# Feed-forward stage: the output tiles of the former block placed behind pairs 2 to 5 instead of 3 to 6

## The chip, the cores and the metric

One core of a Trainium2 chip runs the kernel. The metric is the device time of one execution in microseconds (us). PE is TensorE, DVE is VectorE, ACT is ScalarE, POOL is GpSimd and SP is SyncE, whose queue starts the transfers.

## What is computed

Two layers over 4096 tokens of 512 features, each with an attention part and a feed-forward part and a residual sum and layer norm behind each. The change touches only the first layer's feed-forward part and what is interleaved with it:

```python
ff_gate = _qdot(x, w_gating[0])            # 512 -> 2048, fp8 operands
ff1 = _qdot(x, w_gating[1])                # 512 -> 2048
activations = gelu(ff_gate) * ff1
outputs = _qdot(activations, w_linear)     # 2048 -> 512
x = _layernorm(x + outputs)                # called x2 below
q, k, v = x @ Wq + bq, x @ Wk + bk, x @ Wv # second layer's attention
```

## The kernel before, in words

The program has four stages, written as four functions; each engine runs one stage after the other. The change is in `stage_b` (the feed-forward part of layer 0 together with the projections of layer 1). It works on 8 blocks of 512 tokens. The hidden dimension of 2048 is cut into 16 tiles, taken in 8 pairs.

For block i, pair j, PE has two jobs of eight 512-column fp8 matmuls (L981): `g` (gate half) and `u` (up half). ACT copies g out of PSUM (L848), squares it (L851), later applies tanh (L857), and copies u out (L854). DVE does eight operations per pair, in which those of pair j are interleaved with the second half of pair j-1; the last one writes `b_act` in fp8 (step `a8`, L930). So the last activation of block i-1, a8(i-1, 7), is made during pair 0 of block i.

Beside the pairs of block i PE has jobs of former blocks:

- `x` (L972): two groups of eight transposes of the next block's input. ACT writes them out in fp8 (L862).
- `y` (L988): four output tiles of block i-1, sixteen fp8 matmuls each, which need all of its activations. ACT copies a tile out (L866), DVE adds the residual (L935) and takes its statistics (L939, L943). Behind the fourth tile DVE makes `var` (L946), POOL the power (L833), DVE `nb` (L949), and ACT the four `norm` (L871), in place in x2.
- `x2` (L994): two groups of eight transposes of the normed block i-2; ACT makes the high part (L876), DVE the low part (`xl`, L953).
- `K`, `Q`, `VT` (L142 to L144): twelve 512-column matmuls each on these parts; ACT and DVE write them out (L880, L958, L884). `V` (L999) is four transposes back.

The order of PE's jobs is a list written out by hand, in L704 to L726. `between[j]` stands between g and u of pair j, `beside[j]` behind u. The orders of ACT and DVE are derived from this list (L729 to L770): each job appends its own steps, in order. One rule there matters: the fourth output tile puts four norms into a list, and **the next g step appends two of them behind its own copy and square, the next u step appends the other two behind its tanh and its copy** (L738, L743). Every engine works its queue strictly in this order.

PSUM has eight banks. `g`, `u`, `x` and `x2` take two banks each and go round three such places in order of the list (L784); so each waits until the job three places before it in this sequence has been read out. `y`, `K`, `Q`, `VT` and `V` alternate between banks 6 and 7. The steps that free a place are g's copy for g (L848), u's copy for u (L854), L862 for x and `xl` for x2.

For a block 3 or later the job list of before is: g0 VT u0 V, g1 u1 x2-0, g2 x2-1 u2 K, g3 u3 y0, g4 u4 y1, g5 u5 y2, g6 u6 y3, g7 x-0 x-1 u7 Q.

Of the kernel before, what the change touches and what calls it, by code (L numbers as in the profile page):

```python
# [663 lines left out]
def stage_b(nc, whole, a, bank, psum, const, prev, high, high32, low, low32, early, w8g_dram, w8l_dram, kqv, x1_dram, x2_dram):  # L664
# [4 lines left out]
    with ExitStack() as stack:  # L669
# [29 lines left out]
        chunks = range(CH)  # L699
# [5 lines left out]
        for i in range(NB):  # L705
            beside = {j: [] for j in range(pairs)}
            between = {j: [] for j in range(pairs)}
            if i >= 3:
                between[0] = [("VT", i - 3)]
                beside[0] = [("V", i - 3)]  # L710
            if i >= 2:
                beside[1] = [("x2", i - 2, 0)]
                between[2] = [("x2", i - 2, 1)]
                beside[2] = [("K", i - 2)]
                beside[7] = [("Q", i - 2)]
            if i >= 1:
                for c in chunks:
                    beside[3 + c] = [("y", i - 1, c)]
            if i + 1 < NB:
                between[7] = [("x", i + 1, 0), ("x", i + 1, 1)]  # L720
            for j in range(pairs):
                order += [("g", i, j)] + between[j] + [("u", i, j)] + beside[j]
# [10 lines left out]
        for name in order:  # L733
# [17 lines left out]
            elif kind == "y":  # L751
                c = name[2]
# [919 lines left out]
def program(nc, a, out):  # L1672
# [9 lines left out]
    with ExitStack() as stack:  # L1682
# [19 lines left out]
        kqv["Ql"], Ql32 = twins(nc, stack, "Ql", [P, NB, BT])  # L1702
        kqv["V"] = s.sb("V", [P, NB, BT], F32)
        B = stage_b(nc, stack, a, bank, psum, const, A, high, high32, low, low32, flat32, w8g_dram, w8l_dram, kqv, x1_dram, x2_dram)
        C = stage_c(nc, stack, a, bank, const, B, high32, low32, flat, flat32, kqv, x2_dram)
        D_ = stage_d(nc, stack, s, a, bank, const, C, flat, flat32, kqv, Ql32, out_blocks)
# [86 lines left out]
```

## Time and profile before

| what | value |
|---|---|
| median of 3 runs | 1659.33 us (1655.27 to 1660.53) |
| profiled execution | 1657.51 us, its span 1655.8 us |
| mean granted PE clock over the span | 0.971 |
| busy: PE, DVE, ACT, POOL | 92%, 62%, 44%, 21% |
| feed-forward stage | from 670 us to about 1147 us |
| a block of it in the steady state | about 58.3 us |

Busy time is what an engine spent in instructions. Matmul durations overlap, so starts are read and not durations: eight matmuls of g start 0.22 us apart and take 1.73 us of PE, though their line says 1.89. In a timeline, the bracket at the end of a line gives the idle time of that engine just before and what ended it.

### The profile page before, as it was taken

To read this page: it belongs to the slowest core of one execution; us is meant where nothing else is said; L and a number is where in the kernel's file an instruction comes from. 1 tells how busy PE (TensorE), PEld (TensorE's weight loads), DVE (VectorE), ACT (ScalarE), POOL (GpSimd) and SP (SyncE) were. 2 spreads that over 40 slices of the span, in tenths; PEclk is the share of its full clock that TensorE was granted. 3 is DMA by queue.
4 is the path that set the end of the run, shared out by engine and by line. 5 is a ranking of instruction groups with operands and counts; after the bars stand their busy time and mean duration, and the time that the engine had idled before them with its cause. 6 is when DMAs were issued, how large, how long until landed. Compare 5 with 4: busy or idle time off the path is not lost.

```text
span 1655.8 us, 24158 instructions
## 1 busy us (share of the span) xinstructions
PE 1522.2 (92%) x9681; PEld 1050.0 (63%) x9681; DVE 1031.6 (62%) x1993; ACT 722.6 (44%) x1005; POOL 344.8 (21%) x256
## 2 busy tenths in 40 slices
PE   8899999999999987898999999988888999998998
PEld 6777777777777766444545554545655656666887
DVE  3335445454445455697777768673699888655665
ACT  3332323323333322687767767762233333333333
POOL 0011212121112122100000000000356677760001
PEclk9999999999999999999999999998999999999999
DMA  6111221202020140101001101001300000000112
GB/s 221 33 41 35 66 58 43 76 25 76 25 76 25 55 153 33 39 1 51 26 26 52 51 1 51 1 28 62 88 1 1 0 1 1 1 1 14 64 52 77
DMA packets 43483, 71.51 MB, mean 43 GB/s; under 512 B 7035, under 2 KB 14715, under 8 KB 43244
## 3 DMA queue, kind: packets, MB, share of 16 engines
q1 hardware_dynamic: 43372, 69.97, 12.6%
q8 instruction: 77, 1.26, 0.3%
q14 instruction: 34, 0.28, 0.1%
HBM read 44.80 MB, written 25.17 MB: 42 GB/s over the span
## 4 chain that ended last, share of the span: by engine, by line
PE 58%; issue 23%; DVE 11%; ACT 3%; POOL 3%; DMA 0%; DVEq 0%; POOLq 0%; ACTq 0%
PE psum L142 11%; PE psum L144 11%; PE psum L143 11%; PE psum L1319 5%; PE psum L640 2%; PE psum L635 2%; PE psum L629 2%; PE psum L649 2%; PE psum L614 2%; DVE c_mx L1235 1%; PE psum L981 1%; PE psum L988 1%; PE psum L1297 1%; POOL c_ls L1174 1%; PE psum L653 1%
## 5 line engine op out<-in xcount | busy, mean ns | idle before, releaser
L981 PE MATMUL psum<-early,high 128*128 128x512 fp8e4 x1024 | 240.8, 387 | 23.1 <-DVE low_r L953 15.8
L981 PEld LDWEIGHTS psum<-early,high 128*128 128x128 fp8e4 x1024 | 98.9, 99 | 147.0 <-DVE low_r L953 17.2
L406 POOL TENSOR_TENSOR rms<-ms,mhalf 128x16 f32<-128x16 f32 x32 | 95.0, 2967 | 428.3 <-DVE ms L476 428.3
L1174 POOL TENSOR_TENSOR c_ls<-c_ls,c_pr 128x512 f32<-128x512 f32 (+2 forms) x136 | 161.4, 1187 | 62.8 <-ACT c_pr L1211 54.1
L1211 ACT ACTIVATE c_pr<-c_sc 128x512 f32<-128x512 f32 (+2 forms) x144 | 85.3, 594 | 172.6 <-DVE c_sc L1255 157.5
L142 PE MATMUL psum<-Qh,Kh 128*128 128x512 f32 (+1 forms) x272 | 142.2, 523 | 1.8 <-DVE Ql_r L1528 1.8
L1319 PE MATMUL psum<-c_pr,V 128*128 128x512 f32 (+2 forms) x288 | 139.1, 565 | 4.0 <-ACT c_pr L1211 3.8
L1255 DVE TENSOR_TENSOR c_sc<-psum,c_mb 128x512 f32<-128x512 f32 (+2 forms) x144 | 91.9, 641 | 45.7 <-PE psum L144 34.6
L988 PE MATMUL psum<-high,b_act 128*128 128x512 fp8e4 x512 | 115.2, 379 | 0.0
L142 PE MATMUL psum<-early_r,high_r 128*128 128x512 f32 x256 | 105.6, 413 | 2.6 <-DVE early_r L439 2.6
L565 ACT ACTIVATE early<-psum 128x512 f32<-128x512 f32 x64 | 38.3, 598 | 157.4 <-PE psum L144 157.4
L144 PE MATMUL psum<-Qh,Kl 128*128 128x512 f32 (+1 forms) x272 | 105.8, 389 | 0.0
L833 POOL TENSOR_TENSOR b_rstd<-b_var,mhalf 128x4 f32<-128x4 f32 x8 | 8.1, 1009 | 453.2 <-DVE b_var L946 453.2
L144 PE MATMUL psum<-early_r,low_r 128*128 128x512 f32 x256 | 100.2, 392 | 0.0
L143 PE MATMUL psum<-early_r,high_r 128*128 128x512 f32 x256 | 99.9, 390 | 0.0
L1235 DVE TENSOR_REDUCE c_mx<-psum 128x1 f32<-128x512 f32 (+2 forms) x144 | 89.1, 636 | 4.7 <-PE psum L1300 4.7
L467 DVE TENSOR_TENSOR sm<-psum,keep 128x1024 f32<-128x1024 f32 x64 | 75.2, 1218 | 24.1 <-PE psum L629 24.1
L988 PEld LDWEIGHTS psum<-high,b_act 128*128 128x128 fp8e4 x512 | 50.0, 98 | 60.4 <-issue 0.3
L848 ACT ACTIVATE early<-psum 128x1024 bf16<-128x1024 f32 x64 | 65.4, 1023 | 48.0 <-PE psum L981 47.9
L457 DVE SCALAR_TENSOR_TENSOR qf<-psum,small,early 128x1024 f32<-128x1024 f32 x16 | 19.8, 1279 | 84.5 <-PE psum L614 84.5
L473 DVE TENSOR_REDUCE ms<-ot 128x16 f32<-128x512 f32 x32 | 21.9, 683 | 80.9 <-ACT ot L525 80.1
L142 PEld LDWEIGHTS psum<-Qh,Kh 128*128 128x128 f32 x272 | 52.1, 191 | 30.0 <-issue 14.4
(243 smaller groups left out, 3432.2 us busy)
## 6 DMA issues: line engine op xcount, KB each, us to landing
low<-x_dram SPq DMA_DIRECT2D x9, 1024.0 KB, 5.6
xs<-in_L_attn_x SPq DMA_DIRECT2D x8, 1024.0 KB, 7.9
wst<-in_L_ffn_w_gating SPq DMA_DIRECT2D x16, 512.0 KB, 4.4
x_dram<-xs SPq DMA_DIRECT2D x7, 1024.0 KB, 4.9
x_dram<-low SPq DMA_DIRECT2D x5, 1024.0 KB, 4.3
wst<-in_L_ffn_w_linear SPq DMA_DIRECT2D x16, 256.0 KB, 4.6
high<-x_dram SPq DMA_DIRECT2D x4, 1024.0 KB, 6.6
out<-high SPq DMA_DIRECT2D x4, 1024.0 KB, 4.3
```

Of the source, the lines that this page charges most:

```text
L142: tensor.matmul(out, hi_w, hi_x, start=first, stop=False, skip_group_check=True)
L143: tensor.matmul(out, hi_w, lo_x, start=False, stop=False, skip_group_check=True)
L144: return tensor.matmul(out, lo_w, hi_x, start=False, stop=last, skip_group_check=True)
L406: nc.gpsimd.tensor_tensor(rms[:, :], ms[:, :], const["mhalf"][:, 0:H], ALU.pow).then_inc(*done)
L467: v.tensor_tensor(sm[:, c % 2, two, :, :].rearrange("p j g t -> p (j g) t"), psum[:, two, :].rearrange("p j (g q) -> p (j g) q", g=DC), tr ...
L981: last = t.matmul(out[:, h, :], w8g[:, tile + k, (2 * m + h) * P:(2 * m + h + 1) * P], x8[:, u, k, :], start=k == 0, stop=k == DC - 1)
L988: last = t.matmul(out[:, :], act8[:, u, h, m * P:(m + 1) * P], w8l[:, h // 2, (h % 2) * D:(h % 2 + 1) * D], start=h == 0, stop=h == HC - 1)
L1174: nc.gpsimd.tensor_tensor(ls[:, i % 2, q0:], ls[:, i % 2, q0:], pr[:, g % SLOTS, q0:], ALU.add).then_inc(*L.done(*name))
L1211: nc.scalar.activation(pr[:, g % SLOTS, q0:], sc[:, g % SLOTS, q0:], ACT.Exp, scale=scale).then_inc(*A.done(*name))
L1235: nc.vector.tensor_reduce(mx[:, i % 2, q, k:k + 1], bank[bank_of[name]][:, 0:n], AX_X, ALU.max).then_inc(*done)
L1255: nc.vector.tensor_tensor(sc[:, g % SLOTS, q0:], bank[bank_of["s", i, k]][:, q0:], mb[:, i % 2, q0:], ALU.add).then_inc(*done)
L1319: last = nc.tensor.matmul(out[:, q0:], values[:, keys], pr[:, g % SLOTS, q0:], start=k == 0, stop=k == tiles(i) - 1, skip_group_check=True)
```

## The change

The first output tile of the former block moves between the second group of x2 transposes and u2. The other three come behind u3, u4 and u5 rather than u4, u5 and u6. Nothing stands behind u6.

```diff
             if i >= 1:
-                for c in chunks:
-                    beside[3 + c] = [("y", i - 1, c)]
+                between[2].append(("y", i - 1, 0))
+                for c in chunks[1:]:
+                    beside[2 + c] = beside[2 + c] + [("y", i - 1, c)]
```

The list for block 3 or later becomes: g0 VT u0 V, g1 u1 x2-0, g2 x2-1 **y0** u2 K, g3 u3 **y1**, g4 u4 **y2**, g5 u5 **y3**, g6 u6, g7 x-0 x-1 u7 Q. No instruction is added or removed. The lists of ACT and DVE, which are derived, follow: the four norms now stand two behind g6's copy and square and two behind tanh of pair 5 and u6's copy.

## Rows read from the trace of the kernel before

**Rows 1.** The page, part 1: busy us, share of the span, instructions.

```profile
PE 1522.2 (92%) x9681; PEld 1050.0 (63%) x9681; DVE 1031.6 (62%) x1993; ACT 722.6 (44%) x1005; POOL 344.8 (21%) x256
```

**Rows 2.** Waits, 780 to 1070 us: who for whom, total us, times, longest.

```profile
DVE early L903 <- ACT early L851: 30.3, 30, 2.4
...
PE psum L981 <- DVE low_r L953: 13.1, 5, 2.6
```

**Rows 3.** Timeline of PE, block 4, pairs 1 to 3: start, length, what.

```profile
884.02 1.04 PE L994 MATMUL psum<-ident,low 128*128 128x128 f32 x8
...
886.62 1.04 PE L994 MATMUL psum<-ident,low 128*128 128x128 f32 x8
890.28 3.39 PE L981 MATMUL psum<-early,high 128*128 128x512 fp8e4 x8 [2.62 <-DVE low_r L953]
...
893.96 0.39 PE L144 MATMUL psum<-high_r,b_wl 128*128 128x512 f32 x1
...
896.26 3.63 PE L981 MATMUL psum<-early,high 128*128 128x512 fp8e4 x16
```

**Rows 4.** Timeline of DVE and ACT, the same place.

```profile
883.76 0.69 DVE L930 TENSOR_SCALAR b_act<-early 128x1024 fp8e4<-128x1024 bf16 x1
...
886.37 1.02 ACT L876 ACTIVATE high_r<-psum 128x1024 fp32r<-128x1024 f32 x1
...
888.40 0.69 DVE L930 TENSOR_SCALAR b_act<-early 128x1024 fp8e4<-128x1024 bf16 x1
889.01 2.54 DVE L953 TENSOR_TENSOR low_r<-psum,high_r 128x1024 fp32r<-128x1024 f32 x2
```

**Rows 5.** Timeline of PE, block 3 from y3 on, to block 4's g0.

```profile
862.15 3.62 PE L988 MATMUL psum<-high,b_act 128*128 128x512 fp8e4 x16
865.61 1.89 PE L981 MATMUL psum<-early,high 128*128 128x512 fp8e4 x8
867.33 1.91 PE L972 MATMUL psum<-ident,low 128*128 128x128 f32 x16
869.08 1.89 PE L981 MATMUL psum<-early,high 128*128 128x512 fp8e4 x8
...
873.69 1.90 PE L981 MATMUL psum<-early,high 128*128 128x512 fp8e4 x8
```

**Rows 6.** Timeline of ACT, the same place.

```profile
870.29 1.52 ACT L871 ACTIVATE low<-low,b_nb,b_rstd 128x512 f32<-128x512 f32 x2 [0.65 <-DVE b_nb L949]
...
871.72 1.91 ACT L862 ACTIVATE early<-psum 128x1024 fp8e4<-128x1024 f32 x2
...
873.53 1.05 ACT L857 ACTIVATE early<-early 128x1024 bf16<-128x1024 bf16 x1
...
874.48 1.02 ACT L854 ACTIVATE early<-psum 128x1024 bf16<-128x1024 f32 x1
...
875.38 1.52 ACT L871 ACTIVATE low<-low,b_nb,b_rstd 128x512 f32<-128x512 f32 x2
...
876.80 0.68 ACT L880 ACTIVATE Qh<-psum,b_bkq 128x512 fp32r<-128x512 f32 x1
```

**Rows 7.** Timeline of PE: start of block 2, u2 of block 6, V(5) in the tail.

```profile
758.40 7.08 PE L981 MATMUL psum<-early,high 128*128 128x512 fp8e4 x32 [2.72 <-ACT early L862]
...
769.54 1.09 PE L994 MATMUL psum<-ident,low 128*128 128x128 f32 x8 [1.21 <-ACT early L854]
...
1006.73 1.90 PE L981 MATMUL psum<-early,high 128*128 128x512 fp8e4 x8 [2.62 <-DVE low_r L953]
...
1111.90 1.12 PE L999 MATMUL psum<-ident,early 128*128 128x128 f32 x4 [5.45 <-DVE Ql_r L958]
```

**Rows 8.** A stretch each: PE, PEld, DVE, ACT, POOL busy; granted clock, DMA share, GB/s.

```profile
890.00:893.00 3.00, 2.72 (x7) 1.04 (x8) 2.90 (x6) 1.24 (x2) 0.00 (x0) 0.50 0.80 308
...
617.00:624.00 7.00, 6.06 (x44) 4.91 (x45) 4.20 (x5) 0.60 (x1) 0.59 (x2) 0.52 0.01 3
...
632.00:635.00 3.00, 1.00 (x10) 0.79 (x9) 3.00 (x4) 0.60 (x1) 2.75 (x1) 1.00 0.04 12
```

## The prediction

> **What bounds the kernel now.** I read the page's busy shares first: PE is busy for 92% of the span, the next engine for 62% [rows 1]. The move concerns one stage, so next come the waits of the feed-forward stage between 780 and 1070 us. PE waits there on one thing that matters: five times, 2.6 us each, its up half is held by the low part of x2 on DVE. DVE in turn waits on ACT in every pair [rows 2], so neither is the bound. Then the timeline of one block (block 4). PE makes x2-0 at 884.02, g2, and x2-1 at 886.62, which is over at 887.5 (x2-0 took 0.87 until g2). Then it stands until 890.28: u2 goes into the two banks of x2-0 and must wait for `xl` of x2-0 [rows 3]. ACT had made the high part at 886.37 to 887.39, but DVE was in the eight steps of its pair until 889.0, and `xl` of x2-0 ran from 889.01 to 890.28 (half of 2.54) [rows 4]. The bracket says 2.62; by the starts it is nearer 2.8.
>
> The gap has a second cost. The eight matmuls of u2 took from 890.28 to 893.32 instead of 1.73 us, since the granted clock was 0.50, the lower of its two levels, over 890 to 893 [rows 8]. That happened in five of the six blocks that have this gap; the sixth, at 1006.73, ran at full clock with the same 2.62 us gap ahead of it [rows 7].
>
> **Part 1: y0 in the gap.** One output tile is sixteen matmuls, 862.15 to 865.61 = 3.46 us [rows 5]. It needs a8(i-1, 7), which DVE wrote at 883.76 to 884.45, 3 us before x2-1 is over [rows 4]. Its bank was last used by VT of pair 0, long read out. So it starts at 887.5 and ends at 890.95, and `xl` of x2-0 is done at 890.28: u2 does not wait, and it runs at full clock. u2 takes 1.73, so K starts at 892.68, and K takes 12 x 0.23 = 2.77 (ten of its matmuls lie between 893.96 and 896.26). Its operand, the second `xl`, is done at 891.55. So g3 starts at 895.45 with y0 already made, where before it started at 896.26 without: 3.46 + 0.81 = 4.3 us. About 0.1 more comes from V in pair 0, which now waits a little for a late ACT. **4.4 us in a block.** Where the clock did not fall before (block 6 by start, 1006.73) it is 1.5 less, 2.9.
>
> What is queued behind it: on ACT, y0's copy now stands ahead of tanh of pair 1, which it holds from 890.2 to about 891.75; on DVE, y0's 1.5 us of sum and statistics stand ahead of pair 2's steps. DVE waited 2.4 us on ACT in the next pair (the longest in rows 2), so this has cover. If that cover were gone the cost would be at most these 1.5 us.
>
> Block 1 has no x2 and no gap; y0 meets a8(0, 7) almost as it is made, and I cost it at nothing (0 to 0.5). Block 2 has also a wait of 1.21 ahead of x2-1, for the copy of u1, with ACT behind because two norms stood ahead of its first g copy [rows 7]. That wait shrinks by some 1.1, so block 2 gives 5.5. Sum: 5.5 + 4 x 4.4 + 2.9 = **26.0 us gained.**
>
> **Part 2: the norms come one pair earlier.** This is the price. After y3 the chain DVE sum, statistics, var, POOL, nb is the same, and ACT's first norm starts 870.29 - 862.15 = 8.14 us after the start of y3 [rows 5, 6]; call that start S. Before, these 8.14 us were covered: the norms stood behind g7's square, ahead of the two x copies, tanh and u7's copy, and what PE needed next was the x copies for g0. They ended at 871.72 + 1.91 = 873.63 and g0 began at 873.69: already a stop of 0.14 us. Now the norms stand behind g6's square and **ahead of tanh of pair 5 and the copy of u6**. PE's sequence g6 u6 g7 x-0 x-1 u7 goes round three places, so x-1 needs the copy of u6 and u7 needs the copy of g7. By the start-to-start times of ACT [rows 6]: two norms 1.43 (870.29 to 871.72), tanh 0.95 (873.53 to 874.48), a u copy 1.02 long and 0.90 to the next, two more norms 1.42 (875.38 to 876.80). So the copy of u6 ends at S + 8.14 + 1.43 + 0.95 + 1.02 = S + 11.54. PE with no wait would come to x-1 at S + 3.46 (y3) + 3.46 (g6, u6) + 1.72 (g7) + 0.87 (x-0) = S + 9.50. **x-1 waits 2.1 us.** It ends at S + 12.45. The copy of g7 comes behind two norms more: it starts at S + 8.14 + 1.43 + 0.95 + 0.90 + 1.42 = S + 12.84 and ends at 13.86. **u7 waits another 1.45 us**, until S + 13.9. From u7 to the next g0 it was 873.69 - 869.08 = 4.61, less the 0.14: g0 at S + 18.4. Without the waits of before and with one pair more behind y3 it would be 873.69 - 862.15 + 3.46 = S + 15.0. **Loss 3.4 us a block**, in blocks 2 to 6: 17.0.
>
> The Trainium skill (TensorE: Matmul & The Clock Gate, the section on the array's architectural detail) says that ACT and DVE are strictly first in, first out, while PE may only pull weight loads ahead. The rows agree as far as they go: every step above stands in list order. By that rule no later copy slips past a norm, which is what this part rests on.
>
> Block 1 has no Q behind u7, and there g0 already waited 2.72 for the x copies [rows 7]. They now end at S + 16.8 against 11.54 + 3.46 = 15.0: 1.8 lost. In block 7 there is no x, so PE isn't stopped in pair 7, but tanh of pairs 5 to 7 comes later, and V(5), which waited 5.45 us for the low part of Q(5) at the end of DVE's chain [rows 7], waits for it: with three ACT steps out of place I get S + 23.2 against S + 21.4, 1.8 lost. Sum: 17.0 + 1.8 + 1.8 = **20.6 us lost.** Net so far 5.4 us faster.
>
> **Part 3: the clock in pair 7.** In 5.3 us, PE now has two gaps (2.1 and 1.45) and 1.74 us of transposes. The trace doesn't show such a place. From both sides: a gap of 2.7 in pair 7 of block 1 was followed by 32 matmuls at full speed, 7.08 us [rows 7], and one of 2 us within 632 to 635 left the clock at 1.00; cost 0. Gaps of 2.6 halved it five times in six, for 1.3 us of lost matmul time. After a gap of 3.07 the clock stayed low for seven microseconds, 617 to 624, with 6.06 us of work in it [rows 8]; that costs about 2.8. I take 1.3 a block, the value of the gaps of 2.6, as idle time here is 3.5 in all but broken up: 5 x 1.3 plus 0.5 in block 1 (where the x copies hide most) = **7.0 us lost**, bounds 0 and 14.
>
> The skill's same page (section on queue depth-cycling in PSUM) has a rule against this change: short idles between groups of matmuls are enough to swing the clock between its levels. No run here has shown it for two gaps of this form. By it the low clock would come in every block, which is the forecast or the third rival below.
>
> **Sum.** -26.0 + 20.6 + 7.0 = +1.6 us on the profiled 1657.5 (span 1655.8 and 1.7 around it), so 1659.1. The median of the runs, 1659.3, lies 1.8 above that profile; with the same +1.6 I forecast **1661 us**. DMAs: the store of x2 waits for the last norm, the reload of its slot for x2-1; both keep tens of microseconds and no queue is moved past them.
>
> **Rivals.** About 0.3% (5 us) is what a measurement of this kernel can tell from no change.
> First, the **clock holds in pair 7**. For: the 2 us gap above. Against: five falls in six. Time: 1659.3 - 5.4 = 1654. Chance 0.15, about half of it beyond 0.3%.
> Second, **slower: the low clock lasts twice as long.** If it falls early in the first gap, the second gap lies in the low stretch and the clock isn't given back until after Q, as at 617. Place: u7 and Q of blocks 1 to 6. Price 2.8 instead of 1.3 a block, 14 us in all: 1659.3 - 5.4 + 14 = 1668. It decides from about 2 us a block on. For: total idle of 3.5; against: seven-microsecond stretches are rare before. Chance 0.20.
> Third, **the norms don't stop PE**, because the banks are not held by the copies I named or nb comes sooner. Then only part 1 is left: 1659.3 - 26 = 1633. For: ACT has idle time in pairs 3 to 5; against: the list and the sum by steps, and the 0.14 us stop that is there before. Chance 0.06.
> The change not doing what it says, y0 being held by a8 or by `xl` all the same, would be a loss of 1 to 3 us a block more, 1670: chance 0.04, as 3 us of slack stand against it.
> The forecast itself has 0.55.
>
> **Range and chances.** 1652 to 1670 takes in the first and second rivals and leaves out the third and the far tail. Faster by over 0.3%: half of the first rival and the third, 0.14. Slower by over 0.3%: most of the second and the last, and a little of the forecast's upper side, 0.26. Within: 0.60.
>
> **What would show it.** Right: no wait of L981 on L953 in blocks 2 to 7; y0 of 3.46 us there, and u2 of 1.73 behind it; in pair 7 two waits of PE on ACT, about 2.1 us at L972 (for L854) and 1.45 at L981 (for L848), in blocks 1 to 6; granted clock below 1 in pair 7 and not in pair 2; a block of some 58.5 us where it was 58.3. Wrong: no gap in pair 7, a new wait at y0 or K, or a clock in pair 7 at 1.00 throughout or low for 7 us.

## The result: no difference that reaches 0.3%

| kernel | median of the runs | profiled span | clock |
|---|---|---|---|
| before | 1656.97 us (14 runs) | 1655.8 us | 0.971 |
| changed | 1660.91 us (14 runs) | 1656.8 us | 0.969 |

The ratio is 1.0022 with a 95% interval of 1.0014 to 1.0030, so the changed kernel is 2 to 5 us slower. It lies on the slower side of the forecast's middle case. The profiled spans are only 1.0 us apart, since the changed kernel's profile reached block 1 2.3 us earlier (709.99 against 712.32 us), ahead of everything that the change touches; differences within the stage are therefore read from one start to another. In the changed kernel the lines of this stage have moved by one (L981 is L982, L988 is L989, L994 is L995, L972 is L973). The same holds in e2 below; in e1 and e6 they have moved by five, and in e3 and e5 by none.

First the waits of PE between 780 and 1070 us (who for whom, total us, times, longest). The wait of [rows 2] for DVE's low part is gone; there are two new ones, five times each:

```profile
PE psum L973 <- ACT early L855: 9.5, 5, 1.9
PE psum L982 <- ACT early L849: 6.0, 5, 1.2
```

Where the gap of [rows 3] was, the timeline of PE in block 4 now reads:

```profile
882.71 1.04 PE L995 MATMUL psum<-ident,low 128*128 128x128 f32 x8
883.58 1.89 PE L982 MATMUL psum<-early,high 128*128 128x512 fp8e4 x8
885.31 1.04 PE L995 MATMUL psum<-ident,low 128*128 128x128 f32 x8
886.18 3.62 PE L989 MATMUL psum<-high,b_act 128*128 128x512 fp8e4 x16
889.63 1.89 PE L982 MATMUL psum<-early,high 128*128 128x512 fp8e4 x8
...
894.13 3.63 PE L982 MATMUL psum<-early,high 128*128 128x512 fp8e4 x16
```

x2-1, y0, u2 and K follow each other, and u2 takes 1.73 us again. From g0 (872.59) to g3 (894.13) it is 21.54 us with y0 in it; before it was 22.57 without.

And where [rows 5] had no gap, the timeline of PE in block 3, from y3 to block 4's g0:

```profile
851.66 3.62 PE L989 MATMUL psum<-high,b_act 128*128 128x512 fp8e4 x16
855.12 5.34 PE L982 MATMUL psum<-early,high 128*128 128x512 fp8e4 x24
860.30 1.04 PE L973 MATMUL psum<-ident,low 128*128 128x128 f32 x8
863.22 1.21 PE L973 MATMUL psum<-ident,low 128*128 128x128 f32 x8 [1.89 <-ACT early L855]
865.54 3.59 PE L982 MATMUL psum<-early,high 128*128 128x512 fp8e4 x8 [1.11 <-ACT early L849]
872.59 1.90 PE L982 MATMUL psum<-early,high 128*128 128x512 fp8e4 x8
```

x-1 waits for the copy of u6, u7 for the copy of g7, and u7's eight matmuls then last 3.4 us instead of 1.73. ACT's queue in the same place shows why (timeline of ACT; L872 are the norms, L858 is tanh of pair 5, L855 the copy of u6, L849 the copy of g7):

```profile
859.80 1.52 ACT L872 ACTIVATE low<-low,b_nb,b_rstd 128x512 f32<-128x512 f32 x2 [0.64 <-DVE b_nb L950]
861.22 1.04 ACT L858 ACTIVATE early<-early 128x1024 bf16<-128x1024 bf16 x1
862.17 1.00 ACT L855 ACTIVATE early<-psum 128x1024 bf16<-128x1024 f32 x1
863.07 1.51 ACT L872 ACTIVATE low<-low,b_nb,b_rstd 128x512 f32<-128x512 f32 x2
864.49 1.00 ACT L849 ACTIVATE early<-psum 128x1024 bf16<-128x1024 f32 x1
```

The norms start 859.80 - 851.66 = 8.14 us after y3, as they did before. But the two copies that PE needs now stand behind them. The granted clock of two such places (a stretch each; the number behind POOL's busy time is the clock) is 0.51, half speed, behind the gaps of block 3, and 1.00 in block 2, where the same two gaps lie at 806 and 808:

```profile
864.00:871.00 7.00, 5.89 (x17) 3.09 (x16) 4.11 (x9) 6.23 (x7) 0.00 (x0) 0.51 0.40 150
...
806.00:809.00 3.00, 1.75 (x12) 1.17 (x12) 2.60 (x5) 2.97 (x4) 0.00 (x0) 1.00 0.24 89
```

**The balance by block**, from starts in both timelines. Pairs 0 to 2 (g0 to g3, plus 3.46 us for y0, which is inside now): blocks 2 to 7 gained 5.7, 4.7, 4.5, 4.4, 3.0 and 4.7, in sum 27.0 us. Pairs 6 and 7 (y3 to the next g0, against 11.54 + 3.46): blocks 1 to 6 lost 2.2, 3.4, 5.9, 5.0, 4.7 and 6.1, in sum 27.4. The wait of V(5) in the tail grew from 5.45 to 7.26: 1.8. Together 2.2 us slower. From block 1's g0 to V(5) the two profiles are 399.58 and 401.98 us long: 2.4 apart.

### The profile page after: what moved, and what is told of

It is laid out like the page before. It is cut to its first block, busy times and chain, and to the rows that moved or that the text cites. A ratio compares the mean times of both kernels' runs of the same rounds, so it can differ in the third digit from the quotient of the medians.

```text
span 1656.8 us, 24158 instructions
## 1 busy us (share of the span) xinstructions
PE 1522.7 (92%) x9681; PEld 1051.9 (63%) x9681; DVE 1032.2 (62%) x1993; ACT 724.3 (44%) x1005; POOL 344.6 (21%) x256
## 4 chain that ended last, share of the span: by engine, by line
PE 58%; issue 23%; DVE 11%; ACT 4%; POOL 3%; DMA 0%; POOLq 0%; DVEq 0%; ACTq 0%
PE psum L142 12%; PE psum L144 11%; PE psum L143 11%; PE psum L1320 5%; PE psum L640 2%; PE psum L635 2%; PE psum L629 2%; PE psum L649 2%; PE psum L614 2%; DVE c_mx L1236 2%; PE psum L989 1%; PE psum L1298 1%; PE psum L982 1%; PE psum L653 1%; POOL c_ls L1175 1%
## 5 line engine op out<-in xcount | busy, mean ns | idle before, releaser
L982 PE MATMUL psum<-early,high 128*128 128x512 fp8e4 x1024 | 240.6, 388 | 11.8 <-ACT early L849 7.6
L982 PEld LDWEIGHTS psum<-early,high 128*128 128x128 fp8e4 x1024 | 99.4, 99 | 137.1 <-issue 13.3
L989 PE MATMUL psum<-high,b_act 128*128 128x512 fp8e4 x512 | 115.2, 379 | 0.0
L989 PEld LDWEIGHTS psum<-high,b_act 128*128 128x128 fp8e4 x512 | 49.9, 98 | 59.2 <-issue 0.6
L849 ACT ACTIVATE early<-psum 128x1024 bf16<-128x1024 f32 x64 | 65.3, 1021 | 49.3 <-PE psum L982 49.2
```

The lines of the kernel that those rows point to most:

```text
L982: last = t.matmul(out[:, h, :], w8g[:, tile + k, (2 * m + h) * P:(2 * m + h + 1) * P], x8[:, u, k, :], start=k == 0, stop=k == DC - 1)
L989: last = t.matmul(out[:, :], act8[:, u, h, m * P:(m + 1) * P], w8l[:, h // 2, (h % 2) * D:(h % 2 + 1) * D], start=h == 0, stop=h == HC - 1)
```

## The experiments

**Are the early norms the cause?** In e1 the order of the tiles is the changed one, and the norms wait in their list until pair 7.

```diff
             elif kind == "g":
-                act_order += [("g16", *name[1:]), ("sq", *name[1:])] + norms[:2]
-                norms = norms[2:]
+                act_order += [("g16", *name[1:]), ("sq", *name[1:])]
+                if name[2] == pairs - 1:
+                    act_order += norms[:2]
+                    norms = norms[2:]
 ...
-                act_order += [("u16", *name[1:])] + norms
-                norms = []
+                act_order += [("u16", *name[1:])]
+                if name[2] == pairs - 1:
+                    act_order += norms
+                    norms = []
```

> The new order of output tiles, with one rule put back: the four norms stand behind g7's square and u7's copy, as before the change, though y3 is a pair earlier. My theory (the gap in pair 2 is worth 26 us, the norms ahead of tanh and of u6's copy cost what is lost): both waits of pair 7 gone, u2 without a gap, 26 us under the kernel before, about 1631 us. Rival (the loss comes from the output tiles lying earlier as such, or the gain of part 1 is given back elsewhere): time within 0.3% of the kernel before, with waits in pair 7.

Measured: 1631.52 us against 1657.21 of before, ratio 0.9852 (0.9831 to 0.9874). The stretch 780 to 1060 us of this kernel (PE, PEld, DVE, ACT, POOL busy, clock) has no idle time on PE at all and a full clock:

```profile
780.00:1060.00 280.00, 280.00 (x1376) 151.61 (x1375) 225.72 (x430) 218.85 (x249) 5.05 (x5) 1.00 0.09 31
```

In before the same stretch has 269.42 us of busy PE at 0.98, in the changed kernel 264.52 at 0.96. ACT in e1, in the order u6's copy, g7's copy, square, norms, x copies:

```profile
854.50 1.00 ACT L859 ACTIVATE early<-psum 128x1024 bf16<-128x1024 f32 x1
855.40 1.01 ACT L853 ACTIVATE early<-psum 128x1024 bf16<-128x1024 f32 x1
856.45 1.06 ACT L856 ACTIVATE early<-early 128x1024 bf16<-128x1024 bf16 x1
857.41 1.51 ACT L876 ACTIVATE low<-low,b_nb,b_rstd 128x512 f32<-128x512 f32 x2
858.82 1.91 ACT L867 ACTIVATE early<-psum 128x1024 fp8e4<-128x1024 f32 x2
```

No norm waits for `nb` any more, since it has been there for a while. The early tiles as such cost nothing; the loss was in the place of four ACT instructions. The early norms also had one small good side: in block 2 e1 gains 4.5 us in pairs 0 to 2 and not 5.7, because the wait of 1.2 us ahead of x2-1 [rows 7] is back once the norms stand where they stood before. The rival falls.

**Is it enough to move y0 alone?**

```diff
                 for c in chunks[1:]:
-                    beside[2 + c] = beside[2 + c] + [("y", i - 1, c)]
+                    beside[3 + c] = beside[3 + c] + [("y", i - 1, c)]
```

> From the changed kernel: y0 stays between x2-1 and u2, but y1 to y3 stand behind pairs 4 to 6, as before the change, so nothing stands behind u3 and the norms fall behind g7's square and u7's copy without any new rule. My theory: as e1, 25 to 26 us under the kernel before, as DVE's 4.0 us of pair 3 against PE's 3.45 is covered by the pair behind it. Rival (the early tiles matter, not the norms): the same time as e1 could not come from this order, it would lie between.

Measured: 1631.56 us, ratio 0.9845 (0.9826 to 0.9864), which is e1's time. PE has no wait between 780 and 1045 us. So the part of the change that brought the gain is y0, and the move of the other three tiles brought the early norms and, by time, nothing else.

**Do the parts add up?** e3 has the early norms, and the gap back.

```diff
-                between[2].append(("y", i - 1, 0))
-                for c in chunks[1:]:
+                for c in chunks:
                     beside[2 + c] = beside[2 + c] + [("y", i - 1, c)]
```

> From the changed kernel: y0 stands behind u2 and K rather than between x2-1 and u2; y1 to y3 as in the changed kernel. So the gap of pair 2 is back and the early norms stay. My theory (the parts add up): the changed kernel's time plus 26 us, about 1685 us, with the 2.6 us wait for xl in blocks 2 to 7 and the two waits of pair 7 in blocks 1 to 6. Rival (the time lost in pair 7 is the gap of pair 2 moved on, work that has to wait somewhere): no more than 5 us above the changed kernel.

Measured: 1683.35 us, ratio 1.0155 (1.0133 to 1.0177): 26 us above before, but only 22.4 above the changed kernel, where I had 26. PE's waits from 700 to 1175 us name all three gaps:

```profile
PE psum L981 <- DVE low_r L953: 15.8, 6, 2.7
PE psum L972 <- ACT early L854: 12.6, 7, 1.9
...
PE psum L981 <- ACT early L848: 6.9, 6, 1.2
```

The missing part is mostly the clock. The gap of pair 2 is the same 2.6 us in all six blocks, but here it was followed by slow matmuls in three of them only, where before it was five. Two of e3's six, eight matmuls of u2 each:

```profile
839.30 1.90 PE L981 MATMUL psum<-early,high 128*128 128x512 fp8e4 x8 [2.62 <-DVE low_r L953]
...
1024.80 3.40 PE L981 MATMUL psum<-early,high 128*128 128x512 fp8e4 x8 [2.62 <-DVE low_r L953]
```

By the traces, the clock was at its lower level for 24 us in the changed kernel's blocks and for 31 in e3's; half of the difference, 3.4, with six gaps of 2.8 makes 20, near the 20.5 us by which the two profiles differ between block 1's g0 and V(5). The rival (a gap that only moves on, at most 5 us above the changed kernel) falls: the waits add, and what each costs in clock does not add exactly.

**What is the clock worth?** Two kernels fill gaps with useless matmuls, so the waits stay and only the idleness goes. e4 does it in pair 7 of the changed kernel, e7 in pair 2 of the kernel before:

```diff
+                if (kind == "x" and b >= 3 and name[2] == 1) or (kind == "u" and 2 <= b < NB - 1 and name[2] == pairs - 1):
+                    q = ("Q", b - 3) if kind == "x" else ("Q", b - 2)
+                    wait_for(pe, 0, free[q])
+                    for r in range(9 if kind == "x" else 6):
+                        t.matmul(bank[bank_of[q]][:, :], w8g[:, r % DC, 0:P], x8[:, (b - 1) % 2 if kind == "x" else b % 2, r % DC, :], start=True, stop=True, skip_group_check=True)
```

> The changed kernel with useless work in the two gaps of pair 7, blocks 2 to 6: nine 512-column fp8 matmuls ahead of x-1 and six ahead of u7 into the bank that Q uses next (75 in all, 16 us of PE time). The waits for ACT stay, only PE isn't idle in them. My theory (about 8 us of the loss are the clock, which falls for idleness): granted clock 1.00 in pair 7, and 8 us less than the changed kernel, though 75 matmuls are added. Rival (the low clock comes from something else, or costs nothing): the changed kernel's time or up to 16 us more.

Measured: 1653.08 us, ratio to before 0.9976 (0.9965 to 0.9988): 7.8 us under the changed kernel with 75 matmuls more. PE in block 3 (L971 is the filler):

```profile
860.88 2.10 PE L971 MATMUL psum<-early,high 128*128 128x512 fp8e4 x9
862.94 1.09 PE L978 MATMUL psum<-ident,low 128*128 128x128 f32 x8
863.86 1.46 PE L971 MATMUL psum<-early,high 128*128 128x512 fp8e4 x6
865.26 1.90 PE L987 MATMUL psum<-early,high 128*128 128x512 fp8e4 x8
```

x-1 and u7 start no earlier, 2.94 and 5.26 us after x-0 (2.92 and 5.24 in the changed kernel), but u7 is at full speed: the granted clock over 780 to 1060 us is 1.00, where the changed kernel has 0.96.

```diff
+                if kind == "u" and b >= 2 and name[2] == 2:
+                    wait_for(pe, 0, free["K", b - 2])
+                    for r in range(12):
+                        t.matmul(bank[bank_of["K", b - 2]][:, :], w8g[:, r % DC, 0:P], x8[:, u, r % DC, :], start=True, stop=True, skip_group_check=True)
```

> The kernel before with useless work in the gap of pair 2, blocks 2 to 7: twelve 512-column fp8 matmuls ahead of u2, 2.6 us, into the bank that K uses next (72 in all, 15.5 us). u2 still waits for xl. It separates the two terms of part 1. My theory: about 17 us of the 26 are the gap itself and some 7 are the clock behind it; so the granted clock stays at 1.00 in pair 2, and the kernel is 6 to 8 us faster than before with 72 matmuls added. Rival (the clock is not part of that gain): the time of the kernel before or above.

Measured: 1648.03 us, ratio 0.9942 (0.9926 to 0.9958): 9.1 us under before, somewhat more than I had expected, with an interval that just reaches into 6 to 8. In blocks 2 to 7 the clock did not fall. By the starts of g0 and g3 in the two profiles e7 gains 1.7, 1.7, 1.5, 1.3, 0.0 and 1.7 us in these blocks, some 7.8 in sum, and nothing in the one block where the clock had held before. So of part 1's 26 us 8 to 9 are clock and 17 to 18 are the gap itself, and the rival falls for both places.

**Does the place in ACT's queue decide which job waits?** e5 puts all four norms behind u6's copy.

```diff
             elif kind == "g":
-                act_order += [("g16", *name[1:]), ("sq", *name[1:])] + norms[:2]
-                norms = norms[2:]
+                act_order += [("g16", *name[1:]), ("sq", *name[1:])]
```

> The changed kernel with all four norms behind u6's copy, none behind g6's square. By the sum of steps x-1 does not wait, and g7's copy stands behind four norms: norms from about S + 9.3, copy of g7 done at S + 13.2, so u7 waits once, 2.8 us, and g0 comes at S + 17.7 plus clock (S is the start of y3). My theory: a loss of 2.7 in place of 3.4 us a block before the clock, total 0 to 7 us under the changed kernel. Rival (the two waits come from nb and not from the places in ACT's queue): the same two waits and the same time as the changed kernel.

Measured: 1652.55 us, ratio 0.9973 (0.9961 to 0.9986), 8.4 under the changed kernel, a little beyond what I had. The waits of PE from 700 to 1175 us:

```profile
PE psum L981 <- ACT early L848: 15.5, 6, 2.6
```

One wait of 2.6 us in the place of two, for g7's copy, as the sum of steps has it. So the order in ACT's queue decides which job waits. `nb` had a small share of its own in the changed kernel, the 0.64 us in which ACT stood idle ahead of the first norm; here the norms start without a wait. From block 1's g0 to V(5) e5's profile is 6.8 us shorter than the changed kernel's (395.15 against 401.98), within what I had. Where the clock held (block 2), y3 to g0 takes 17.63 us against 18.40, as forecast. Only some 1.6 of the 6.8 us are clock, and the rest is shorter waits. The clock fell behind five of the six gaps, but each time for some 3.4 us, 1.7 us of loss in each of blocks 3 to 6, and never for the seven that blocks 3 and 6 of the changed kernel had.

**A better tail.** e6 is e1 and one more edit:

```diff
-        order += [("VT", b - 2), ("V", b - 2)] + [("x2", b - 1, k) for k in range(2)] + [("K", b - 1), ("Q", b - 1)]
+        order += [("VT", b - 2)] + [("x2", b - 1, k) for k in range(2)] + [("V", b - 2), ("K", b - 1), ("Q", b - 1)]
```

> e1 with one more edit in the tail: V(5) stands behind the two groups of x2(6) transposes rather than ahead of them, so these run while V waits for the low part of Q(5). Expected: K(6) no longer waits 2.5 us for xl behind them, 3 to 4 us less than e1. If DVE's queue sets K's start anyway, the same time as e1.

Measured: 1628.17 us, ratio 0.9816 (0.9794 to 0.9839), the fastest here. That is 3.4 under e1, but the two intervals overlap, so by time alone it is not settled. The two profiles bear it out: from block 1's g0 to V(6) it is 407.4 us in e1 and 403.8 here. The waits in its tail (1060 to 1120 us) are shorter: V(5) waited 5.1 us in e1 and 3.0 here, K 2.5 and 1.2.

```profile
PE psum L1004 <- DVE Ql_r L963: 3.0, 1, 3.0
PE psum L142 <- DVE low_r L958: 1.2, 1, 1.2
```

## Why the prediction held, point by point

**Part 1, gap of pair 2.** Forecast 4.4 us a block, 2.9 where the clock had held, 5.5 in block 2, 26.0 in sum. Measured 4.4 to 4.7, 3.0 and 5.7, in sum 27.0. e2, which has only this part, is 25.7 us faster by time; by the starts of g0 and g3 its profile gains 24.8. The difference to 26 is mostly one item that stood in the wrong part of the sum: the 1.1 us of block 2 come from the early norms, so they belong to part 2, and e1 and e2 don't have them.

**Cover on ACT and DVE.** y0's copy and sums stood ahead of pair 1's tanh and pair 2's steps, as feared; e2 and e1 show no wait of PE behind it. It was free.

**Part 2, the norms.** Forecast: x-1 waits 2.1 and u7 1.45, loss 3.4 before the clock. Block 2, where the clock held, gives the clean figure: y3 at 794.46, g0 at 812.85, so 18.39 us against the forecast's 18.4. In e4, whose clock holds, blocks 2 to 6 all take 18.4. By starts x-1 waits 2.05 us and u7 1.45; the brackets say 1.9 and 1.2, shorter than by starts, like the 2.62 of [rows 3]. The tail: V(5) came at y3 + 23.25 where I had 23.2.

**ACT's strict order.** The Trainium skill (TensorE: Matmul & The Clock Gate, the section on the array's architectural detail) calls ACT's queue strictly first in, first out. The rows of ACT above agree: the copy of u6 was possible from about 859 us, when u6 was done, and began at 862.17, behind norms that waited for `nb`.

**Part 3, the clock: the term that was mis-sized.** I had 7.0 us, 1.3 a block. Measured, as the rest above block 2's 18.39: 2.5, 1.6, 1.3 and 2.7 in blocks 3 to 6, nothing in block 2, 0.4 in block 1: some 8.6. e4 gives 7.8 for blocks 2 to 6 by time. The rival of the long stretch was right in two blocks of six (3 and 6, seven microseconds each), the rival of the holding clock in one. The forecast's mean was near because both came true in part; the rows gave no way to tell which block would go which way, so that the sum fits so well is partly luck. The Trainium skill (TensorE: Matmul & The Clock Gate, the section on queue depth-cycling in PSUM) says of another kernel that short idles between groups of matmuls swing the clock. This case bears it out with gaps of 1.9 and 1.2 us, 0.9 us of transposes between them, in five of six blocks.

**Sum.** Forecast +1.6 us, measured +2.2 by blocks in the profiles (+2.4 from start to start) and +3.6 by the ratio. Its interval, 2.3 to 5.0, takes in the second of these and not the forecast's 1.6, so the change is somewhat slower than forecast. That the forecast of 1661 us meets the measured 1660.91 is luck: it started from a median of 1659.33 us for the kernel before, of three runs, and fourteen runs give 1656.97. The 2.4 us too much there and the 2 too little in the change cancel.

## What to carry to other kernels

Where the lists of the other engines are derived from the order of one, moving a job moves all that hangs on it: read off, for every queue, what comes to stand ahead of what, and price that before the gap that is to be filled. Work that nobody needs soon (here four norms, which PE's transposes first read some twenty microseconds later: 859.80 to 882.71 us in the changed kernel) belongs behind the copies that free PSUM, not where its producer happens to end. A rearrangement that measures as next to nothing can be a gain of 26 us and a loss of 29, and one part of it alone is the kernel that was wanted.

## What was not expected of the hardware

Useless matmuls in a gap made the kernel faster twice, by 7.8 us with 75 of them and by 9.1 us with 72. Whether a gap costs clock is no property of the gap alone: the same 2.6 us in pair 2 halved the clock in five of six blocks before and in three of six in e3, and the same pair of gaps in the changed kernel cost between 0 and 2.7 us. The traces do show what goes with the length of a low stretch, though. In the two costly blocks of the changed kernel the clock had fallen well before u7 began; in block 5 it fell shortly before. A stretch each, with u7 at 865.54 in block 3 and at 984.14 in block 5:

```profile
864.00:865.00 1.00, 0.44 (x3) 0.08 (x1) 1.00 (x3) 1.00 (x2) 0.00 (x0) 0.53 0.00 0
...
983.00:984.00 1.00, 0.00 (x0) 0.00 (x0) 1.00 (x3) 1.00 (x2) 0.00 (x0) 0.76 0.00 0
```

In before, the changed kernel, e3, e4 and e5 the clock fell 24 times at such gaps of pairs 2 and 7. Four times it fell 1.1 to 1.9 us ahead of the u job and stayed low for 6.8 us. The other 20 times it fell at most 0.6 us ahead, or only after u had begun, and stayed low for 3.4 us. Why it falls in one block and not in another, and when, was not tried and stays open.
